# Row statistics moved into the cross layer and the routing chain cut into three parts, in a two-layer decoder kernel

## The reference

```python
x = x + _L0_attn_ref(_layernorm(x), ...)
x = x + _L0_xattn_ref(_layernorm(x), ctx_2048, ...)   # self part and cross part over 375 context rows
x = x + _L0_ffn_ref(_layernorm(x), gate_w, w1, w2, w3, sw1, sw2, sw3, expert_bias)
x = x + _L1_attn_ref(_layernorm(x), ...)
x = x + _L1_xattn_ref(_layernorm(x), ...)
x = x + _L1_ffn_ref(_layernorm(x), ...)
```

```python
scores = softmax(xf @ gate_w)                        # 1792 tokens x 8 experts
_, sel = top_k(scores + expert_bias, 2)
top_scores = take_along_axis(scores, sel, axis=1)
counts = bincount(sel.reshape(-1), length=8)
order = argsort(sel.reshape(-1), stable=True)
routed_in = xf[order // 2] * top_scores_sorted[:, None]
h = silu(ragged_dot(routed_in, w1, counts)) * ragged_dot(routed_in, w3, counts)
routed_out = ragged_dot(h, w2, counts)
out = silu(xf @ sw1) * (xf @ sw3) @ sw2
out = out.at[order // 2].add(routed_out)
```

## Time and profile before

| | us |
|---|---|
| median of three timed runs | 3577.09 |
| lowest and highest | 3573.23, 3577.46 |
| profiled execution, its own time | 3581.59 |
| its span | 3579.9 |
| TensorE busy in the span | 3306.0 (92%) |
| VectorE busy | 2438.5 (68%) |
| ScalarE busy | 1733.2 (48%) |
| GpSimd busy | 798.9 (22%) |

### The profile page before, as it was taken

How to read it: one execution, slowest core, us unless ns; L and a number is a source line. 1 busy time by engine, 2 the same in 40 slices (tenths; PEclk the granted TensorE clock), 3 DMA queues, 4 the chain that set the end, 5 groups by cost and what they waited for, 6 DMA issues and landing times. The chain is left out here.

```text
span 3579.9 us, 54783 instructions
## 1 busy us (share of the span) xinstructions
PE 3306.0 (92%) x18088; PEld 2673.1 (75%) x18088; DVE 2438.5 (68%) x6424; ACT 1733.2 (48%) x4171; POOL 798.9 (22%) x901
## 2 busy tenths in 40 slices
PE   5858998996999999999999978999989889988999
PEld 4637877885787787778778856888878767767887
DVE  5987888885666766756666666899755555558332
ACT  5974454443344334443443432788547654541222
POOL 1003443442322222332222223000323310000000
PEclk9879999998999999999999988999999989999999
DMA  6130010001000000200000015999810134423000
GB/s 230 29 76 14 0 47 24 0 32 69 20 21 28 20 21 28 92 21 21 20 28 20 20 64 203 357 404 398 305 43 1 48 114 123 126 91 106 11 10 21
DMA packets 113587, 296.14 MB, mean 83 GB/s; under 512 B 37921, under 2 KB 42017, under 8 KB 107665
## 3 DMA queue, kind: packets, MB, share of 16 engines
q1 hardware_dynamic: 107264, 276.39, 21.9%
q0 software_dynamic: 6160, 17.67, 1.6%
HBM read 251.65 MB, written 41.68 MB: 82 GB/s over the span
## 5 line engine op out<-in xcount | busy, mean ns | idle before, releaser
L40 PE MATMUL bank<-w,cross_ctx_part 128*125 128x512 f32 x1536 | 516.3, 417 | 8.1 <-DVE cross_qn L1091 4.7
L40 PEld LDWEIGHTS bank<-w,cross_ctx_part 128*125 128x125 f32 x1536 | 281.9, 187 | 93.1 <-DVE cross_kn L1091 14.7
L1001 ACT ACTIVATE cross_prob<-bank,cross_neg_max 112x375 f32<-112x375 f32 x256 | 146.9, 574 | 359.2 <-DVE cross_neg_max L1097 359.2
L40 PE MATMUL bank<-w_low,cross_ctx_part 128*125 128x512 f32 x768 | 303.6, 395 | 0.0
L1097 DVE TENSOR_REDUCE cross_neg_max<-bank 112x1 f32<-112x375 f32 x256 | 134.0, 524 | 197.5 <-PE bank L873 194.8
L40 PE MATMUL bank<-moe_wt,moe_zT 128*128 128x448 f32 x1176 | 265.6, 375 | 2.1 <-DVE moe_zT L1727 1.5
L1717 DVE TENSOR_TENSOR moe_wt<-moe_raw,moe_wt 128x1792 fp32r<-128x1792 f32 (+1 forms) x111 | 232.0, 2107 | 16.3 <-ACT moe_wt L1615 15.2
L40 PE MATMUL bank<-w,self_xq 128*112 128x512 f32 x512 | 213.9, 418 | 23.0 <-DVE w_low L596 23.0
L40 PEld LDWEIGHTS bank<-moe_wt,moe_zT 128*128 128x128 f32 x1176 | 216.3, 191 | 17.8 <-issue 1.7
L40 PE MATMUL bank<-mlp_zT,mlp_signs 128*128 128x448 f32 x1024 | 220.6, 368 | 5.6 <-DVE mlp_zT L2407 5.6
L40 PEld LDWEIGHTS bank<-mlp_zT,mlp_signs 128*128 128x128 f32 x1024 | 193.4, 189 | 27.2 <-issue 5.9
(11 more groups left out here) (404 smaller groups left out, 8223.1 us busy)
## 6 DMA issues: line engine op xcount, KB each, us to landing
moe_raw<-in_moe_w SPq DMA_DIRECT2D x74, 896.0 KB, 7.6
moe_raw<-in_moe_w SPq DMA_DIRECT2D x37, 1024.0 KB, 8.6
stream<-in_L1f SPq DMA_DIRECT2D x32, 768.0 KB, 7.9
cross_ctx_raw<-in_ctxT SPq DMA_DIRECT2D x32, 750.0 KB, 4.2
wide_ctxT<-in_ctxT SPq DMA_DIRECT2D x16, 750.0 KB, 4.2
wide_ctx_rows<-in_ctx SPq DMA_DIRECT2D x16, 750.0 KB
expert_rows<-a_zeros SPq DMA_DIRECT2D x1, 8960.0 KB, 25.6
moe_zrow<-expert_rows SPq DMA_DIRECT2D x35, 256.0 KB, 7.8
```

The source lines that it names most:

```text
L40: mm = pe.matmul(out, a, b, start=first and n == 0, stop=last and n == len(pairs) - 1)
L1001: op = act.activation(prob[:, t % SLOTS, i, :], score_bank(t)[0:S, i * NK:(i + 1) * NK], ACT.Exp, bias=neg_max[:, h:h + 1], accum_out=tota ...
```

## The change

Three edits, and what goes with them:

1. A new buffer `row_stats` holds the statistics of each sequence. In each step of the cross layer's second half from the third on, VectorE measures one sequence of x right after `add_out`: sequences 0 to 13. The expert layer measures only 14 and 15 (`measure_last`), and `spread_of` turns the statistics of four sequences into mean and variance.
2. The routing chain stands in three parts: the choices; then the low part of tile 1's rows, tile 0's multiplication and chunk 2's low part; then the counts; then tile 0's hidden low part; then the rest. The four small products move from tile 0 into tile 1, behind its U. Scaled rows begin after tile 1's multiplication instead of tile 0's, so each group of seven comes one tile later.
3. Tile 0's rows are turned before the last logits product, and ScalarE takes them before the last logits.

```diff
+            def measure_row(b):
+                dve.wait_ge(s["x_done"], B + b + 1)
+                dve.bn_stats(k.row_stats[0:S, bass.ds(b, 1), :].rearrange("p b n -> p (b n)"),
+                             x[:, bass.ds(b, 1), :].rearrange("p b d -> p (b d)")).then_inc(s["row_stat"], 1)
...
                         add_out(b - 1, base)
+                    if base == B:
+                        measure_row(b - B - 2)
                     for t in range(NS):
...
+MEASURED = B - 2
...
-                if i < 2:
+                if i == 0:
+                    pe.wait_ge(s["chain"], 2)
+                if i == 1:
                     pe.wait_ge(s["places_ready"], 1)
...
+            pe.wait_ge(s["z_low"], 13)
+            transpose_rows(0)
             route_logits(3)
...
-            transpose_rows(0)
             for i in range(TILES):
                 rise(i, "U", 1, "silu_ready", "up_in_psum")
-                if i + 1 < TILES:
-                    transpose_rows(i + 1)
-                rise(i, "G", 3, "h_ready", "gate_in_psum")
-                if i == 0:
+                if i == 1:
                     pe.wait_ge(s["tables_ready"], 8)
...
+                if i + 1 < TILES:
+                    transpose_rows(i + 1)
+                rise(i, "G", 3, "h_ready", "gate_in_psum")
                 if i:
                     fall(i - 1)
...
+            rows_high(0)
             act.wait_ge(s["logitsT_in_psum"], 4)
...
-            rows_high(0)
             act.wait_ge(s["chain"], 2)
...
-            def measure(g):
+            def measure_last():
+                for b in range(MEASURED, B):
+                    dve.bn_stats(k.row_stats[0:S, b, :], x[:, b, :]).then_inc(s["stat"], 1)
+
+            def spread_of(g):
+                if g == 3:
+                    dve.wait_ge(s["stat"], B - MEASURED)
                 for b in range(4 * g, 4 * g + 4):
-                    dve.bn_stats(stats[:, b, :], x[:, b, :]).then_inc(s["stat"], 1)
-                for b in range(4 * g, 4 * g + 4):
-                    dve.wait_ge(s["stat"], b + 1)
-                    dve.bn_aggr(k.mean_var[0:S, b, :], stats[:, b, :]).then_inc(s["centre"], 1)
+                    dve.bn_aggr(k.mean_var[0:S, b, :], k.row_stats[0:S, b, :]).then_inc(s["centre"], 1)
...
-            measure(0)
-            measure(1)
+            spread_of(0)
+            spread_of(1)
+            spread_of(2)
             for b in range(0, 4):
                 normalise(b)
-            measure(2)
+            measure_last()
+            spread_of(3)
...
-            measure(3)
...
+            rows_low(1)
+            gated(0)
+            split_low(2)
             after(dve.tensor_tensor(both[:, 8:, :], chosen[:, 0], chosen[:, 1], ALU.add))
...
                 dve.tensor_tensor(sums[1][:, 8:, :], sums[0][:, 8:, :], sums[0][:, 0:B, :], ALU.add).then_inc(s["counted"], 1)
-            rows_low(1)
-            split_low(2)
+            hidden_low(0)
...
-                if i:
+                if i > 1:
                     hidden_low(i - 1)
...
-                gated(i)
+                if i:
+                    gated(i)
...
-                while rows_done < min(2 * B, 7 * (i + 1)):
+                while i and rows_done < min(2 * B, 7 * i):
                     scale_rows(rows_done)
```

More of the change, by code:

```diff
@@ L70, in __init__ @@
         self.mean_var = self.sb(ctx, "mean_var", [P, B, 2], F32)
+        self.row_stats = self.sb(ctx, "row_stats", [P, B, 6], F32)
         self.rstd = self.sb(ctx, "rstd", [P, B], F32)
@@ L643, in normed_attention @@
              "inverse", "probs_ready", "probsT_in_psum", "probsT_ready", "cat_in_psum", "cat_scaled", "cat_clipped",
-             "cat_exponent", "cat_magic", "cat_shifted", "cat_rounded", "y_in_psum", "x_done", "x_landed")
+             "cat_exponent", "cat_magic", "cat_shifted", "cat_rounded", "y_in_psum", "x_done", "row_stat", "x_landed")
     s = {n: k.sem(f"{name}_{n}") for n in names}
```

## The result

| | before | after |
|---|---|---|
| median of 20 runs, us | 3576.59 | 3581.99 |
| lowest and highest | 3571.91, 3579.97 | 3577.85, 3591.53 |
| profiled execution, its own time | 3581.59 | 3581.0 |
| its span | 3579.9 | 3579.0 |

The ratio of the medians' runs is 1.0018 with a 95% interval of 1.0011 to 1.0025: the medians differ by 5.4 us, the interval is 3.9 to 8.9. That is clear of noise, but a change under 0.2% counts as none here. So stages have to be compared, not spans.

The account below looks back on a forecast made before the run. TensorE bounds almost everywhere, but scatters set when the sparse tiles begin. Cross layer 0.6, tile 7's turning 0.9 and clock 2.0 give +3.5 on 3577.1, so 3580.6 us; 8 in 10 for 3571 to 3587.

Parts of the forecast that it names:

- The mechanism: Start of the sparse tiles: scatters set it, a lead in tiles 0 to 6 is worth nothing, the clock behind waits costs.
- The opening: Expert layer's start: routing chain 4.35 us sooner, tile 0's hidden rows turned 13 us sooner, 6.9 us wait at tile 4.
- Last scatter +0.9, T of tile 7 +0.9: Expert layer: the last scatter, and with it the turning of tile 7's rows, comes 0.9 us later, at 2236.6.
- The clock, +2.0: TensorE behind its 11 us wait for tile 7's rows: lower clock costs 1.95 us in the first product, 0.1 in turning.
- The cross steps, 0 and +0.6: Cross layer's second half: the added statistic costs 0 in each of 13 looped steps and 0.6 us in the last.
- rival C: Cross steps: statistics stand on their chain, up to 0.61 us in each of 13; +11.4, 3588.5 us; chance 0.14.
- The sparse stalls, 0 or less: Start of the sparse tiles: an earlier split of chunks 3 and 4 may remove a small stall; 0, bounds -0.7 and 0.
- Rival A: Expert layer: scatters run without a hole, tile 7's rows are turned 5.8 us sooner; -3.2, 3573.9 us; chance 0.18.
- B: Turning of tile 7's rows: not held by scatters, so TensorE's 8 us lead stays; -7.4, 3569.7 us; chance 0.07.
- D: TensorE's opening: tile 0's hidden rows still wait for the whole routing chain; +0.6, 3577.7 us; chance 0.06.

Follow-up runs that it names:

- e9: Changed kernel scaling and scattering only 16 of the 32 rows, all products kept; ratio 0.9957 to the kernel before.
- e4: Changed kernel with tile 7's rows turned behind tile 6's second product up and tile 5's product down; ratio 0.9988 to the kernel before.
- e7: Changed kernel with 36 matmuls that nobody reads ahead of the turning of tile 7's rows; ratio 0.9996 to the kernel before.
- e1: Changed kernel without statistics in the cross layer, all sixteen sequences measured in the expert layer's opening; ratio 1.0001 to the kernel before.
- e2: Changed kernel with the row loads of tiles 4 and 5 issued ahead of the five weight chunks; ratio 0.9997 to the kernel before.
- e3: Changed kernel with each group of scaled rows one tile sooner, as before the change; ratio 0.9991 to the kernel before.
- e10: The kernel before, without edits, profiled on another chip; one run without a ratio, last cross step 26.08 us.

## Why the prediction was right, and where not

- *The mechanism* was right: T of tile 7 hangs on the line of scatters, the lead of the first tiles is waited away there, and the clock behind the wait costs more. e9 shows the first for that line as a whole, e4 the second, e7 the third.
- *The opening.* Routing chain at 33.25 behind the last addition, tile 0's H 7.2 us behind it (7 forecast), a wait of 6.74 at T of tile 4 (6.9), scatter 14 at 2203.65 (2204.15), T of tile 7 at 2236.11 (2236.6).
- *Last scatter +0.9, T of tile 7 +0.9.* The scatter came +1.7 later counted from the layer's start, as one took 2.37 us; the rows of tile 7 then landed sooner, 8.96 us behind the last scatter instead of 10.61. T moved by +0.09. Two errors, +0.8 and -1.6, of which one half cancels the other.
- *The clock, +2.0:* measured +1.53 in the first profile, 1.5 to 2.7 in the others with a wait of 7 to 11 us.
- *The cross steps, 0 and +0.6:* the mis-sized terms. The last step paid 1.17 (1.6 to 1.7 against e1): the statistic's own 0.55 as forecast, the rest as the clock's return comes later. The looped ones paid 0.03 each for the statistic, which VectorE's and TensorE's idle time did not fully swallow, and 0.04 in both halves for something in the new build that no term held; its cause is open. Together 2.5 instead of 0.6. The 0.28 per step from which rival C would decide was far off.
- *The sparse stalls, 0 or less:* +1.23 in the first pair, but on the other chips 10.16 before and 10.02 after. The wait is for a weight chunk while the DMA engines are busy throughout (1.01 to 1.05 of their time in four profiles); it varies from run to run, so its sign was a guess, and that it makes the sum below meet the medians is luck.
- *The sum:* 0.6 + 0.9 + 2.0 = 3.5 forecast, 2.53 + 0.09 + 1.53 + 1.23 = 5.4 found. The range held (3582 in 3571 to 3587), and so did "no change". Two of the prediction's own signs came out just outside: looped steps of 38.67 us instead of 38.5 to 38.6, which it had named as a sign of being wrong, and a last scatter at 2227.15, 2.05 us from 2225.1 instead of within 2.
- *Rival A* (scatters without a hole) fell by the rows it was weighed with: the hole at scatter 14 was there. e2 and e3, which narrow it to 2.45 and 1.25 us, show what that brings: 1.6 and 3.7 us at T of tile 7. *B* fell by the wait of 11.12 us there, and *D* by H of tile 0, which came 13.5 us sooner behind the last addition than before.

## What to carry to other kernels

Ask of every gain in time where the next engine will wait; if that place is held by another line (here 32 scatters through one engine), move work into the wait, or behind it, before shortening what stands ahead. A short instruction that is nearly free in a loop (0.03 us a step here) can cost its whole length in the last step, where nothing of a next one covers it. Look behind the stage before calling a gain or a loss of the clock final: here 0.9 of 1.7 us in the last step came back in the next stage. And compare kernels stage by stage: two profiled executions differed by 6 us in code that nobody changed.

## What the runs showed of the hardware

- After the same 6.14 us wait TensorE's clock came back after 7, 9, 10 or 13 of sixteen products. It was 13 in all eight profiles with the statistic ahead of the maximum (last step 27.36 to 27.41 us), 7 in the four without (25.70 to 25.78), 10 and 9 in the two of the kernel before (26.23 and 26.08). The clock's return is worth up to 1.2 us at a place whose code is untouched, and where it came after 7 or 9, the first product of the next stage had ten slow matmuls of twelve instead of three to five. TensorE here in the kernel without statistics (e1):

```profile
2123.92 0.63 PE L40 MATMUL bank<-wo,cross_catq 128*112 128x512 f32 x1
2124.34 0.48 PE L40 MATMUL bank<-wo_low,cross_catq 128*112 128x512 f32 x1
2124.66 0.39 PE L40 MATMUL bank<-wo,cross_catq 128*112 128x512 f32 x1
```

- Two waits of 1.62 and 1.24 us (2614 to 2618 us before, 2617 to 2621 after) were followed by some 6 us at the lower clock in one execution and by none in the other.
- ScalarE waits that the program does not explain appear on three chips while tiles 2 to 5 run, in both kernels, and not on the first. After TensorE's product had ended ScalarE stood for another 1 to 8 us at a time, 7 to 16 us in all in each kernel but e9. The DMA engines are at 1.02 of their time in e10's longest (2194 to 2200 us) and at 0.50 to 0.68 in others; what the cause is stays open.
